# Fused attention and ternary feed-forward kernel: second norm from sums, a reordered opening, right-tap products on ScalarE and other moves in the last slots

## The chip, the cores and the metric

The kernel runs on 1 core of a Trainium2 chip. The metric is the device time of one execution in microseconds (us). PE is TensorE, DVE is VectorE, ACT is ScalarE, POOL is GpSimd and SP is the engine that issues all DMAs here.

## The reference, cut to what matters

```python
# x: (4, 2048, 512) float32, ctx: (4, 154, 512), 16 heads of 32, hidden width 2048
x = x + xattn(layernorm(x), ctx, ctx, Wq, bq, Wk, bk, Wv, bv, Wo, bo)  # causal mask, key > query is masked
x = x + ffn(layernorm(x), w1, conv_w, conv_b, w2)

def act_quant(x):
    scale = 127.0 / clip(max(abs(x), axis=-1), 1e-05)
    return clip(round(x * scale), -128, 127) / scale
def weight_quant(w):
    scale = 1.0 / clip(mean(abs(w)), 1e-05)
    return clip(round(w * scale), -1, 1) / scale
def ffn(x):
    h = act_quant(x) @ weight_quant(w1).T        # 512 -> 2048
    h = depthwise_conv1d(h, conv_w, pad=1) + conv_b   # 3 taps along the sequence
    h = silu(h)
    return act_quant(h) @ weight_quant(w2).T     # 2048 -> 512
```

## The kernel before, in words

The 8192 rows are cut into 16 blocks of 512 (`NB = 16`, four per batch). A software pipeline runs over slots `s = -1 .. 17`. In slot `s` the kernel makes the first norm and the queries of block `s + 1` (`do_q`), the attention, the output projection, the residual and the second norm of block `s` (`do_a`), the first feed-forward product, the three taps and Silu of block `s - 1` (`do_f`), and the second feed-forward product and result of block `s - 2` (`do_m`). Each engine has its own instruction list in program order; the lists are written out by hand, and counted semaphores tie them together. No planner orders anything.

A slot has a tile loop over 16 hidden tiles of 128 channels (`c = 0 .. 15`). For each tile PE multiplies (`mm1`, L867), DVE turns the bank into float32 (`dequant`, L1575), ACT copies the two edge columns and makes the left tap (`neighbours`, `tap0`, L1263), DVE adds the middle tap (`taps`, L1650), and the right tap is a product and a sum on POOL (L642, L644) or, for a few tiles, one DVE instruction (L1654). `TAP` and `SCALE` say which tiles go to POOL. The ring `g` has four buffers, so `dequant(c)` waits for the right tap of tile `c - 4`. PE fills the loop with the scores (L830, L836) and the products with the values (L861) of the attention; ACT has the exponentials (L1244).

Behind the loop comes the tail of the slot, with which the change deals. PE projects the queries (L679), turns the attention output (`turn_o`, L949), projects it (`project_out`, L959; four row tiles, one after another), turns the maxima of Silu (`turn_pm`, L1021), and makes the second product of block `s - 2` (`mm2`, L1043). DVE makes the low halves of the attention output (`at_low`, L1713), the maxima over the hidden tiles (`absmax`, L1659), and then for each of four row tiles `residual` (L1720) with its `bn_stats` (L1723) and `bn_aggr` (L1725). ACT centres each tile (`centre`, L1325) and DVE takes its largest absolute value (`centred_max`, L1729). `norm2` adds epsilon, POOL raises to the power -1/2 (L658), and `quantise` makes the scales in some ten instructions on 4 columns. `scales2` makes the scales of the second product from `turn_pm`; `spread_scales` (L1027) and `r2_copy` spread them, and POOL multiplies (`scaled`, L654) while ACT rounds (`rounded`, L1165). ACT quantises the rows (`hlq`, L1425).

DVE then makes the low halves of the queries (`q_low`, L1696), two results (`result`, L1777) and 16 maxima of the query scores (`maximum`, L1738), one for each `query_scores` of PE (L978). Among these 16 steps PE puts the rest of `mm2`. The slot ends with `turn_xq` (L1004), `spread_row` (L1013) and the first two tiles of `mm1` for the next slot. `offset` preloads a bank of the second product (ACT).

```python
def turn_pm():
    pe.wait_ge(pm_ok, at(s, 3, 2 if s == NB else 0))
    if do_a:
        pe.wait_ge(x2_ok, at(s, TT, 3))
```

In slot -1 the low halves of the queries alternate on DVE with the absolute sums of the weights `w1` (`w_abssum`, L1502), whose total PE spreads (`w_sums`, L763). In slot 0 ACT turns the weights `w2` into float16 (`w2_half`) between the centrings. In slot 16 (`s == NB`) the rows at the seams between blocks, 36 of them, are computed once more with their right neighbours in small instructions (`fix_...`); `fix_mm2` (L914) stands on PE right ahead of the last `mm2` in slot 17 (L1145).

## Time and profile before

| | |
|---|---|
| median of 3 runs | 1595.4 us (1593.45 to 1602.17) |
| profiled execution, its own time | 1609.67 us |
| its span in the trace | 1607.9 us |
| mean granted TensorE clock | 0.953 of full speed |
| busy: PE, DVE, ACT, POOL | 1486.2, 1353.2, 1146.0, 1032.0 us |

Busy time is a sum over the span; what one slot waits for is read from the chain of waits, which follows the work that ended last back to what released it. All times in the rows are microseconds from the start of the span, unless marked as mean ns.

### The profile page before, as it was taken

What the parts mean: (1) busy time and instruction counts of PE and PEld (TensorE: products, weight loads), DVE (VectorE), ACT (ScalarE), POOL (GpSimd) and SP (SyncE); (2) the same over time, 40 slices, a digit from 0 to 9 for tenths busy, and PEclk for the clock granted to TensorE, in tenths of its full rate; (3) what the DMA queues carried; (4) which work ended last, traced back from release to release, by engine and by line L of the source; (5) the groups of instructions that cost most, each with busy time, mean ns of one, the idle gap of its engine ahead of it and who ended that gap; (6) DMA issues with size and microseconds to landing.
All of it is one profiled execution on the core that took longest, in us unless ns stands there. A gap on an engine that the chain in (4) does not pass through costs nothing.

```text
span 1607.9 us, 24773 instructions
## 1 busy us (share of the span) xinstructions
PE 1486.2 (92%) x9097; PEld 906.9 (56%) x9097; DVE 1353.2 (84%) x2078; ACT 1146.0 (71%) x2028; POOL 1032.0 (64%) x838
## 2 busy tenths in 40 slices
PE   9799797999999999999999999999999999998776
PEld 6377364746565564747465665647474656655322
DVE  7565788798988989898889889897979898878896
ACT  3445596968688795959587787959586877878552
POOL 4101186768587685858586876858575867868462
PEclk8967799999999999999999999999999999999987
DMA  8540201012130303021220303031310302020000
GB/s 258 138 137 33 67 8 41 27 36 69 27 93 7 93 8 93 8 53 47 52 66 7 93 8 93 8 86 23 67 41 9 91 8 67 8 67 1 30 27 27
DMA packets 80343, 85.21 MB, mean 53 GB/s; under 512 B 29983, under 2 KB 55839, under 8 KB 79709
## 3 DMA queue, kind: packets, MB, share of 16 engines
q1 hardware_dynamic: 80221, 83.62, 19.2%
q8 instruction: 72, 1.18, 0.3%
q14 instruction: 50, 0.41, 0.1%
HBM read 38.74 MB, written 19.42 MB: 36 GB/s over the span
## 4 chain that ended last, share of the span: by engine, by line
PE 40%; DVE 36%; ACT 18%; issue 4%; POOL 3%; DMA 0%; DVEq 0%; ACTq 0%; SPq 0%
PE ps L861 12%; DVE negm L1738 10%; PE ps L867 8%; PE ps L1043 5%; ACT h L1268 4%; DVE r L1659 4%; DVE pm L1659 4%; ACT hqb L1165 3%; ACT h L1263 3%; ACT pexp L1244 3%; PE ps L830 3%; DVE h L1650 3%; DVE xn L1713 2%; DVE xr L1720 2%; PE ps L679 2%
## 5 line engine op out<-in xcount | busy, mean ns | idle before, releaser
L654 POOL TENSOR_TENSOR h<-h,r 128x512 f32<-128x512 f32 x240 | 306.9, 1327 | 102.4 <-ACT r L1165 102.4
L644 POOL TENSOR_TENSOR h<-h,gall 128x512 f32<-128x512 f32 x235 | 344.1, 1464 | 18.4
L642 POOL TENSOR_TENSOR gall<-gall,cw 128x512 f32<-128x512 f32 x235 | 257.5, 1096 | 118.8 <-DVE h L1650 118.8
L1650 DVE SCALAR_TENSOR_TENSOR h<-gall,cw,h 128x512 f32<-128x512 f32 x256 | 265.6, 1040 | 58.2 <-ACT h L1263 58.0
L861 PEld LDWEIGHTS ps<-va,pexp 128*128 128x128 f32 x2048 | 269.7, 198 | 30.1 <-issue 13.1
L861 PE MATMUL ps<-va,pexp 128*128 128x33 f32 x2048 | 267.3, 276 | 0.0
L867 PE MATMUL ps<-xqT,w1T 128*128 128x512 f16 x1024 | 257.7, 382 | 7.7 <-DVE gall L1575 7.4
L1575 DVE SCALAR_TENSOR_TENSOR gall<-ps,bias,srow 128x512 f32<-128x512 f32 x256 | 191.1, 747 | 79.0 <-POOL h L644 48.0
L1043 PE MATMUL ps<-w2T,hqb 128*128 128x512 fp8e4 x960 | 249.8, 390 | 0.0
L1244 ACT ACTIVATE pexp<-ps 128x512 f32<-128x512 f32 x320 | 179.7, 588 | 70.2 <-PE ps L830 27.9
L1263 ACT ACTIVATE h<-gall,cb,cw 128x512 f32<-128x512 f32 x256 | 221.9, 867 | 8.5
L1738 DVE TENSOR_REDUCE negm<-ps 128x4 f16<-128x616 f32 x256 | 186.6, 791 | 17.3 <-PE ps L981 8.4
L1165 ACT ACTIVATE hqb<-h 128x512 f16<-128x512 f32 x276 | 172.3, 683 | 40.3 <-PE ps L1043 23.4
L679 PE MATMUL ps<-hl,WqT 128*128 128x512 f16 x768 | 170.8, 379 | 2.6 <-DVE hl L1692 2.6
L1268 ACT ACTIVATE h<-h 128x512 f32<-128x512 f32 x256 | 155.3, 681 | 12.2 <-POOL h L644 11.9
L959 PE MATMUL ps<-WoT,pexp 128*128 128x512 f16 x512 | 156.0, 381 | 2.9 <-DVE xn L1713 2.9
L867 PEld LDWEIGHTS ps<-xqT,w1T 128*128 128x128 fp8e4 x1024 | 102.1, 112 | 86.3 <-DVE gall L1575 11.6
L1043 PEld LDWEIGHTS ps<-w2T,hqb 128*128 128x128 f16 x960 | 95.7, 100 | 88.6 <-issue 14.4
L1325 ACT ACTIVATE xn<-xr,mv 128x512 f32<-128x512 f32 x64 | 46.2, 722 | 126.9 <-DVE mv L1725 126.6
L978 PE MATMUL ps<-kB,hl 128*128 128x308 f16 x512 | 120.2, 309 | 14.2 <-DVE hl L1696 7.8
L658 POOL TENSOR_TENSOR nw<-nw,mhalf 128x4 f32<-128x4 f32 x16 | 16.3, 1019 | 175.2 <-DVE nw L1748 175.2
L679 PEld LDWEIGHTS ps<-hl,WqT 128*128 128x128 f16 x768 | 74.5, 98 | 91.0 <-issue 7.5
(220 smaller groups left out, 2328.2 us busy)
## 6 DMA issues: line engine op xcount, KB each, us to landing
qs<-hl SPq DMA_DIRECT2D x192, 128.0 KB, 2.6
xr<-in_x SPq DMA_DIRECT2D x16, 1024.0 KB, 5.5
out<-xr SPq DMA_DIRECT2D x64, 256.0 KB
h<-in_L_ffn_w SPq DMA_DIRECT2D x8, 1024.0 KB, 5.5
srow<-in_L_xattn_bo SPq DMA_DIRECT2D x15, 256.0 KB, 3.2
kst<-kh_scratch SPq DMA_DIRECT2D x32, 38.5 KB
xr<-in_ctx SPq DMA_DIRECT2D x1, 1024.0 KB
h<-in_L_xattn_Wk SPq DMA_DIRECT2D x1, 1024.0 KB, 8.4
```

Of the source, the lines that this page charges most:

```text
L642: gp.tensor_tensor(right, right, cw[:, c, 2:3].to_broadcast([P, TB]), ALU.mult).then_inc(c2m_ok, 1)
L644: gp.tensor_tensor(hc(c), hc(c), right, ALU.add).then_inc(c2p_ok, 1)
L654: gp.tensor_tensor(hc(c), hc(c), r2[:], ALU.mult).then_inc(u_ok, 1)
L679: r = mm(bank, a, b_, start=i == 0, stop=i == n - 1, **kw)
L861: r = mm(o, pr[:, t * P:(t + 1) * P], rhs, start=j == 0 and t % 2 == 0, stop=j == J, skip_group_check=True)
L867: r = mm(F[(c + 1) % 2], w1T[:, k, c * P:(c + 1) * P], xqT[:, k, :], start=k == 0, stop=k == KT - 1)
L1043: r = mm(bank, hq(c)[:, i * P:(i + 1) * P], w2T[:, c, :], start=False, stop=c == CT - 1, skip_group_check=late_results(s))
L1165: return nc.scalar.activation(o, i, ACT.Copy, **kw)
L1244: nc.scalar.activation(pexp[:, i % 3, :], A[i % 2], ACT.Exp, scale=1.0 / QS).then_inc(e_ok, 1)
L1263: nc.scalar.activation(hc(c), g[:, c % 4, 0:TB], ACT.Identity, bias=cb[:, c:c + 1], scale=cw[:, c, 0:1]).then_inc(c0_ok, 1)
L1650: ve.scalar_tensor_tensor(out=hc(c), in0=g[:, c % 4, 1:TB + 1], scalar=cw[:, c, 1:2], in1=hc(c), op0=ALU.mult, op1=ALU.add).then_inc(c1_ok, 1)
L1738: ve.tensor_reduce(negm[:, i, k * J:(k + 1) * J].rearrange("p (b e) -> p b e", b=2), banks, AX.X, ALU.max, negate=True).then_inc(mx_ok, 1)
```

## The change

- The second norm: `residual` also writes the sum of each row (`sum2`, an accumulator output); `bn_stats` and `bn_aggr` are gone. ACT centres with the sum, `512 * (mean - x)`, in four different quarters of `xn`, and a new `square` on ACT sums the squares (`sq2`). `norm2` and `quantise` divide by 512.
- DVE's order in the tail: three residuals, a maximum, the fourth residual, a maximum, `scales2`, two maxima; then, from slot 1 on, two `q_low`, `norm2`, two `q_low`, `quantise`. In slot 0 `q_low` stands ahead of the residuals, and eight of the 16 `maximum` ahead of `quantise`. In slot -1 the four `w_abssum` stand ahead of the four `q_low`.
- ACT in slot 0: `w2_half` stands behind the quantising of the rows. `offset` stands at other places among `centre` and `square`.
- Slot 15: `attention(3)`, `turn_o`, `at_high` and `at_low` are made inside the tile loop, in banks `A[0..3]`.
- Slot 16: the right-tap product of 15 tiles is on ACT and the sum on POOL (10 tiles had both on POOL); all 16 `scaled` are on DVE (6 were on POOL); the seam rows come one or two tiles sooner, and `fix_mm2` stands ahead of `turn_pm`, `fix_scales` ahead of `absmax_last`.

The diff, cut to its core (declarations of buffers and semaphores and renamed banks are left out):

```diff
@@ -129,8 +129,8 @@
 nb1 = sb("nb1", [P, TT], F32)
-st2 = sb("st2", [P, TT, 6], F32)
-mv2 = sb("mv2", [P, TT, 2], F32)
+sum2 = sb("sum2", [P, TT], F32)
+sq2 = sb("sq2", [P, TT], F32)
 nw2 = sb("nw2", [P, 4, TT], F32)
@@ -197,7 +200,7 @@
-    return xn[:, 2 + i % 2, :]
+    return xn[:, (i + 2) % 4, :]
@@ -381,8 +384,8 @@
-TAP = Share((0, 1, 2, 3, 4, 5, 6, 8, 9, 10, 11, 12, 13, 14, 15), last=(0, 2, 3, 5, 6, 8, 9, 11, 12, 14))
-SCALE = Share(tuple(range(CT)), last_but_one=(0, 1, 3, 4, 6, 7, 9, 10, 12, 14), last=(1, 4, 7, 10, 12, 14))
+TAP = Share((0, 1, 2, 3, 4, 5, 6, 8, 9, 10, 11, 12, 13, 14, 15), last=tuple(range(CT - 1)))
+SCALE = Share(tuple(range(CT)), last_but_one=(0, 1, 3, 4, 6, 7, 9, 10, 12, 14), last=())
 def early(s):
@@ -632,15 +635,18 @@
                 gp.tensor_tensor(nw1[:, 1, :], nw1[:, 0, :], mhalf[:], ALU.pow).then_inc(pw1, 1)
-            if s == NB and c == 4:
+            if s == NB and c == 3:
                 pool.wait_ge(fx_dve, 3)
...
-                pool.wait_ge(c1_ok, at(s, CT, c + 1 - CT))
                 right = g[:, c % 4, 2:TB + 2]
-                gp.tensor_tensor(right, right, cw[:, c, 2:3].to_broadcast([P, TB]), ALU.mult).then_inc(c2m_ok, 1)
-                pool.wait_ge(c2m_ok, TAP.done(s, c))
+                if s == NB:
+                    pool.wait_ge(c2a_ok, c + 1)
+                else:
+                    pool.wait_ge(c1_ok, at(s, CT, c + 1 - CT))
+                    gp.tensor_tensor(right, right, cw[:, c, 2:3].to_broadcast([P, TB]), ALU.mult).then_inc(c2m_ok, 1)
+                    pool.wait_ge(c2m_ok, TAP.done(s, c))
                 gp.tensor_tensor(hc(c), hc(c), right, ALU.add).then_inc(c2p_ok, 1)
@@ -940,13 +946,13 @@
             for k in range(NG):
-                if k == 2 and do_f:
+                if k == 2 and do_f and s != NB - 1:
                     pe.wait_ge(g_ok, at(s, CT, 0))
...
                 for t in range(TT):
-                    r = tp(OT[k][:, t * P:(t + 1) * P], osb[:, k, t * P:(t + 1) * P], identf[:])
+                    r = tp(obt(s, k)[:, t * P:(t + 1) * P], osb[:, k, t * P:(t + 1) * P], identf[:])
                 r.then_inc(ot_ok, 1)
@@ -955,6 +961,8 @@
             bank = OB[i]
+            if s == NB - 1 and i == 2 and k == 0:
+                pe.wait_ge(g_ok, at(s, CT, 0))
             for n, (a, part) in enumerate(((0, ah), (0, al), (1, ah))):
@@ -1049,6 +1057,8 @@
         for c in range(CT):
+            if s == NB - 1 and c == 14:
+                turn_o()
             if do_f and c >= 2:
@@ -1063,15 +1073,15 @@
                 mm2((c - 8) // 2)
-            if s == NB and c == 9:
+            if s == NB and c == 8:
                 fix_turn()
-            if s == NB and c == 11:
+            if s == NB and c == 10:
                 fix_mm1()
...
                 turn_x(range(KT))
-            if do_a and c == LASTU + 2:
+            if do_a and c == (LASTU + 1 if s == NB - 1 else LASTU + 2):
                 pv(NS - 2)
@@ -1082,7 +1092,7 @@
                 project_q(k)
-            if do_a and k == 1:
+            if do_a and k == 1 and s != NB - 1:
                 turn_o()
@@ -1094,6 +1104,7 @@
             fix_scales()
+            fix_mm2()
         if do_f:
@@ -1145,8 +1156,6 @@
                         r.then_inc(y_ok, 1)
-        if s == NB:
-            fix_mm2()
         if do_q:
@@ -1262,6 +1271,11 @@
+
+        def right_tap(c):
+            act.wait_ge(c1_ok, at(s, CT, c + 1 - CT))
+            right = g[:, c % 4, 2:TB + 2]
+            copy(right, right, scale=cw[:, c, 2:3]).then_inc(c2a_ok, 1)
@@ -1319,10 +1333,16 @@
-            act.wait_ge(ag_ok, at(s, TT, i + 1))
-            if i >= 2:
-                act.wait_ge(za_ok, at(s, TT, i - 1))
-            nc.scalar.activation(centred(i), ring(s)[:, i, :], ACT.Identity, bias=mv2[:, i, 0:1], scale=-1.0).then_inc(zx_ok, 1)
+            act.wait_ge(x2_ok, at(s, TT, i + 1))
+            if i == 2:
+                act.wait_ge(op_ok, at(s, TT, TT))
+            nc.scalar.activation(centred(i), ring(s)[:, i, :], ACT.Identity, bias=sum2[:, i:i + 1],
+                                 scale=-float(D)).then_inc(zx_ok, 1)
+
+        def square(i):
+            act.wait_ge(zx_ok, at(s, TT, i + 1))
+            nc.scalar.activation(osb[:, i, :], centred(i), ACT.Square, scale=1.0 / D,
+                                 accum_out=sq2[:, i:i + 1]).then_inc(sv_ok, 1)
@@ -1348,14 +1368,14 @@
         for c in range(CT + 1):
-            if s == NB and c == 8:
+            if s == NB and c == 7:
                 act.wait_ge(fx_dve, 12)
                 nc.scalar.activation(fxq, fxr, ACT.Copy, bias=HALF, scale=fq[:, 3:4]).then_inc(fx_act, 1)
-            if s == NB and c == 11:
+            if s == NB and c == 9:
                 act.wait_ge(fx_pe, 2)
...
                 copy(fsr, A[1][:, 0:N3]).then_inc(fx_act, 1)
-            if s == NB and c == CT:
+            if s == NB and c == 14:
                 act.wait_ge(fx_dve, 18)
@@ -1370,11 +1390,16 @@
                 tap0(c - 1)
+                if s == NB and c >= 2:
+                    right_tap(c - 2)
             if do_q and do_a and c in (9, 10):
...
                     x_high(k)
+            if s == NB - 1 and c == 15:
+                for k in range(NG):
+                    at_high(k)
             if do_f and do_a and LASTU < c < CT:
@@ -1385,7 +1410,7 @@
                 w_round(1, i)
-        if do_a:
+        if do_a and s != NB - 1:
             for k in range(NG):
@@ -1404,13 +1429,19 @@
                 w_round(0, i)
-        for i in range(TT):
-            if s == 0:
-                w2_half(i)
-            if do_a:
-                centre(i)
-            if late_results(s) and i != 2:
-                offset((0, 1, 2, 2)[i])
+        if do_a:
+            centre(0)
+            if late_results(s):
+                offset(0)
+            centre(1)
+            centre(2)
+            centre(3)
+            if late_results(s):
+                offset(1)
+            for i in range(TT):
+                square(i)
+            if late_results(s):
+                offset(2)
         if s == 1:
@@ -1424,6 +1455,9 @@
                                      scale=qm1[:, 3, i:i + 1]).then_inc(xq_ok, 1)
+        if s == 0:
+            for i in range(KT):
+                w2_half(i)
         if late_results(s):
@@ -1718,11 +1752,7 @@
             ve.scalar_tensor_tensor(out=ring(s)[:, i, :], in0=OB[i], scalar=1.0 / WS, in1=ring(s)[:, i, :],
-                                    op0=ALU.mult, op1=ALU.add).then_inc(x2_ok, 1)
-            dve.wait_ge(x2_ok, at(s, TT, i + 1))
-            ve.bn_stats(st2[:, i, :], ring(s)[:, i, :]).then_inc(bn_ok, 1)
-            dve.wait_ge(bn_ok, at(s, TT, i + 1))
-            ve.bn_aggr(mv2[:, i, :], st2[:, i, :]).then_inc(ag_ok, 1)
+                                    op0=ALU.mult, op1=ALU.add, accum_out=sum2[:, i:i + 1]).then_inc(x2_ok, 1)
@@ -1744,8 +1774,8 @@
         def norm2():
-            dve.wait_ge(ag_ok, at(s, TT, TT))
-            ve.tensor_scalar(nw2[:, 0, :], mv2[:, :, 1], EPS, None, ALU.add).then_inc(ln2, 1)
+            dve.wait_ge(sv_ok, at(s, TT, TT))
+            ve.tensor_scalar(nw2[:, 0, :], sq2[:], 1.0 / D, EPS, ALU.mult, ALU.add).then_inc(ln2, 1)
@@ -1754,7 +1784,8 @@
             dve.wait_ge(za_ok, at(s, TT, TT))
-            ve.tensor_tensor(qm1[:, 0, :], qx[:], nw2[:, 2, :], ALU.mult).then_inc(ln2, 1)
+            ve.scalar_tensor_tensor(out=qm1[:, 0, :], in0=qx[:], scalar=1.0 / D, in1=nw2[:, 2, :],
+                                    op0=ALU.mult, op1=ALU.mult).then_inc(ln2, 1)
             dve.wait_ge(ln2, at(s, 10, 5))
@@ -1764,7 +1795,7 @@
             dve.wait_ge(ln2, at(s, 10, 8))
-            ve.scalar_tensor_tensor(out=qb[:, 0, :], in0=mv2[:, :, 0], scalar=-1.0, in1=qm1[:, 3, :],
+            ve.scalar_tensor_tensor(out=qb[:, 0, :], in0=sum2[:], scalar=-1.0 / D, in1=qm1[:, 3, :],
                                     op0=ALU.mult, op1=ALU.mult).then_inc(ln2, 1)
@@ -1806,15 +1837,22 @@
                 fix_stats()
-            if s == NB and c == 7:
+            if s == NB and c == 6:
                 fix_quantise()
-            if s == NB and c == 14:
+            if s == NB and c == 12:
                 fix_conv()
+            if s == NB and c == 16:
+                fix_absmax()
             if do_q and do_a and c == 0:
...
                 x_low(1)
+            if s == NB - 1 and c == 13:
+                attention(3)
+            if s == NB - 1 and c == 16:
+                for k in range(NG):
+                    at_low(k)
             if do_f and c < CT:
@@ -1830,21 +1868,21 @@
                 w_scales(1)
-            if do_a and c in (4, 7, 10, 14):
+            if do_a and c in ((4, 7, 10) if s == NB - 1 else (4, 7, 10, 14)):
                 attention((c - 4) // 3)
         if s == NB:
+            fix_scales()
             absmax_last(0, 4, pm)
-            fix_absmax()
+            fix_scaled()
             absmax_last(4, 6, r2)
             merge_last(r2, 2)
-            fix_scales()
             absmax_last(6, 8, pexp[:, 0, :])
...
                 w_limit(1, i)
-        if do_a:
+        if do_a and s != NB - 1:
             for k in range(NG):
@@ -1853,26 +1891,39 @@
             merge()
+        if s == 0:
+            for k in range(NG):
+                q_low(k)
         if do_a:
...
             residual(1)
+            residual(2)
             centred_max(0)
-            residual(2)
+            residual(3)
             centred_max(1)
-            residual(3)
-            norm2()
         if do_f:
...
             centred_max(3)
+        if s > 0 and do_q:
+            q_low(0)
+            q_low(1)
+        if do_a:
+            norm2()
+        if s > 0 and do_q:
+            q_low(2)
+            q_low(3)
+        if s == 0:
+            for n in range(8):
+                maximum(n // NG, n % NG)
+        if do_a:
             quantise()
-        if do_q:
+        if s == -1:
             for k in range(NG):
-                if s == -1:
-                    w_abssum(0, k)
+                w_abssum(0, k)
+            for k in range(NG):
                 q_low(k)
-        if s == -1:
             w_scales(0)
@@ -1885,17 +1936,15 @@
         if s == NB:
-            fix_scaled()
+            fix_result()
             for c in SCALE.dve(s):
                 scaled(c)
-        for n in range(TT * NG):
+        for n in range(8 if s == 0 else 0, TT * NG):
             if do_q:
...
             result(3)
-        if s == NB:
-            fix_result()
         if s == NB + 1:
```

## Rows read from the trace of the kernel before

**Rows 1.** The page, busy us (share of the span) xinstructions.

```profile
PE 1486.2 (92%) x9097; PEld 906.9 (56%) x9097; DVE 1353.2 (84%) x2078; ACT 1146.0 (71%) x2028; POOL 1032.0 (64%) x838
```

**Rows 2.** Chain of waits, tail of slot 9: start us, us, what.

```profile
961.80 0.69 DVE xr L1720
...
963.35 0.69 DVE xr L1720
...
977.53 11.38 DVE negm L1738 x16
```

**Rows 3.** Timeline of DVE there: start us, us, instruction [idle before].

```profile
962.52 0.69 DVE L1723 BATCH_NORM_STATS2 st<-xr 128x6 f32<-128x512 f32 x1
...
964.89 0.65 DVE L1729 TENSOR_REDUCE qx<-xn 128x1 f32<-128x512 f32 x1
...
973.49 2.72 DVE L1696 SCALAR_TENSOR_TENSOR hl<-ps,bqc,hl 128x512 f16<-128x512 f32 x4
```

**Rows 4.** Timeline of PE there.

```profile
966.29 0.63 PE L1021 MATMUL ps<-identf,pm 128*128 128x128 f32 x4 [2.09 <-DVE xr L1720]
966.75 7.07 PE L1043 MATMUL ps<-w2T,hqb 128*128 128x512 fp8e4 x32
...
976.36 0.42 PE L978 MATMUL ps<-kB,hl 128*128 128x308 f16 x2
```

**Rows 5.** Timeline of ACT there.

```profile
940.00 1.28 ACT L1268 ACT_TABLE_LOAD   x1
...
963.47 0.72 ACT L1325 ACTIVATE xn<-xr,mv 128x512 f32<-128x512 f32 x1 [5.65 <-DVE mv L1725]
```

**Rows 6.** Windows of slots 9 and 3: busy us of each engine, granted clock, DMA.

```profile
966.20:974.00 7.80, 7.71 (x40) 4.05 (x41) 7.32 (x25) 1.95 (x4) 1.02 (x1) 1.00 0.01 3
...
432.50:441.10 8.60, 8.60 (x35) 3.63 (x33) 8.12 (x27) 1.93 (x3) 1.02 (x1) 0.80 0.00 0
```

**Rows 7.** Timelines of DVE, PE and SP in slot -1.

```profile
63.88 0.75 DVE L1696 SCALAR_TENSOR_TENSOR hl<-ps,bqc,hl 128x512 f16<-128x512 f32 x1 [10.21 <-ACT hl L1319]
64.55 2.28 DVE L1502 TENSOR_REDUCE wsum<-h 128x4 f32<-128x2048 f32 x1
...
72.79 0.59 PE L763 MATMUL ps<-mw,onesf 128*128 128x1 f32 x2 [6.76 <-DVE mw L1506]
...
73.47 7.84 SPq L532 DMA_DIRECT2D qs<-hl  x12
```

**Rows 8.** Timelines of ACT and PE, tail of slot 0.

```profile
158.64 1.93 ACT L1165 ACTIVATE hqb<-h 128x2048 f16<-128x2048 f32 x1
...
171.51 3.36 ACT L1425 ACTIVATE osb<-xr,qb,qm 128x512 f16<-128x512 f32 x4 [2.42 <-DVE qb L1770]
...
174.25 1.19 PE L978 MATMUL ps<-kB,hl 128*128 128x308 f16 x4 [7.59 <-DVE hl L1696]
...
189.46 1.89 PE L867 MATMUL ps<-xqT,w1T 128*128 128x512 f16 x8
```

**Rows 9.** Timelines of POOL, PE and DVE, slots 16 and 17.

```profile
1527.40 1.04 POOL L642 TENSOR_TENSOR gall<-gall,cw 128x512 f32<-128x512 f32 x1 [2.73 <-DVE h L1650]
1528.52 1.62 POOL L644 TENSOR_TENSOR h<-h,gall 128x512 f32<-128x512 f32 x1
...
1555.98 1.03 PE L867 MATMUL ps<-xqT,w1T 128*128 128x512 f16 x4
...
1566.11 4.40 DVE L1668 TENSOR_REDUCE pm<-h 128x512 f32<-128x4096 f32 x1
...
1573.13 0.69 DVE L1673 TENSOR_TENSOR pm<-pm,r 128x512 f32<-128x512 f32 x1
...
1582.79 5.48 PE L914 MATMUL ps<-w2T,xn 128*12 128x512 fp8e4 x16
...
1583.01 12.72 DVE L1744 TENSOR_TENSOR h<-h,r 128x512 f32<-128x512 f32 x10 [2.54 <-ACT r L1165]
...
1589.17 13.99 PE L1145 MATMUL ps<-w2T,hqb 128*128 128x512 fp8e4 x64
```

11 lines of the change are left out of this document (6 added, 5 removed).

## The prediction

> **What bounds the kernel now.** I began with the page: PE is busy for 92% of the span and DVE for 84% [rows 1], so no engine alone is the limit, and what counts is where PE stands still. The chain of waits over one slot in the middle comes next. It runs on PE through the tile loop, passes to ACT and DVE at its end, and stays on DVE from `at_low` to the last `maximum`. In the tail of slot 9 it steps from residual to residual, 1.55 us apart (961.80 to 963.35), and reaches the first of 16 query maxima at 977.53, 15.7 us after the first residual [rows 2]. The timelines of the engines say what PE does meanwhile: 2.09 us of standstill ahead of `turn_pm`, released by the third residual at 966.29, then 7.07 us of `mm2`, and the first query scores at 976.36 [rows 4]. ACT waits 5.65 us for the first centring [rows 5]. So the tail is DVE's, and PE has its largest hole there; 13 slots (2 to 14) have this tail. The windows show a second price: the stretch of `mm2` in slot 9 has a granted clock of 1.00 (2.4 GHz), that of slot 3 has 0.80, a part of it at 1.2 GHz, behind the same standstill [rows 6]. I asked for that window in slots 2 to 14; six of the 13 (3, 6, 7, 10, 11, 14) look like slot 3.
>
> The median of the runs is 1595.4 us, the profiled execution took 1609.67 (span 1607.9): 14.3 above the median. I make the sum against the profiled one and take it off the median too.
>
> **Steady tail, slots 2 to 14.** Removed from DVE: four `bn_stats` of 0.69 us [rows 3] with `bn_aggr` and their waits. A residual alone takes 0.68 to 0.69, so 1.55 - 0.68 = 0.87 each, 3.5 in all [rows 2]. Added to DVE: the accumulator output of four residuals. No row shows one. It is bounded below by nothing and above by another pass as long as `bn_stats`, 0.69; I take 0.1, since the sum goes along with a pass that runs anyway, so 0.4 in all. DVE would start its maxima 3.1 earlier, at 974.4.
>
> PE: `turn_pm` waits for the third residual. Three residuals follow each other without a break now, done at 961.80 + 3 x 0.78 = 964.1, and PE has finished `project_out` at 966.29 - 2.09 = 964.2. So the standstill goes, and the first scores come at 976.36 - 2.09 = 974.3, done at about 974.6. Each side would have held the other before 974.4 to 974.6. The maxima start at 974.6 in place of 977.53: 2.9 us. Their 16 steps (11.38 us [rows 2]) keep pace with PE, so the end of the slot moves by as much. I take 2.6, because POOL starts to scale only 2.1 earlier and so works 0.8 further into the next slot, and `norm1` waits there for its power on POOL.
>
> The cover of what is added: ACT gets four squares. With 0.72 each, as a centring [rows 5], and the last residual at 965.4, centring, offset and squares end at 965.4 + 0.72 + 0.6 + 2.9 = 969.6; the power on POOL takes 1.0 [rows 6], so `quantise` can begin near 971. DVE is busy to there with `scales2`, two maxima and four `q_low` (2.72 [rows 3]), which were behind it and are now its cover. If each square took 0.3 more, the wait would show by about 1 us. 13 x 2.6 = 33.8 us (bounds 13 x 0.2 = 3, with 0.69 for each accumulator output, and 13 x 2.9 = 38).
>
> On the accumulator output a page has something to say. The Trainium skill ("VectorE: DVE Perf Modes", section "Two Vector instructions with no wait between them") says that an op which writes out its accumulator is two instructions, the main one and a read. No row here shows the second. By it the 0.1 would be the length of a small instruction that overlaps its neighbour, and the sum would stay.
>
> **Clock in six of these slots.** The stretch takes 8.60 against 7.07 [rows 4, 6], 1.5 on PE; about half of it is hidden today because DVE is later anyway. If the clock stays up once the standstill is gone, each of the six gives 0.8 more: 5 us (0 to 9).
>
> **Slot -1.** DVE waits 10.21 us for the first query half and then alternates four `q_low` with three `w_abssum` of 2.28 us; PE stands still for 6.76 [rows 7]. The four sums' weights were asked for on SP long before, right behind the key projections, so the three sums fit into the 10.21, and the queries are complete 3 x 2.28 = 6.8 earlier. What is late next are the 12 query transfers (7.84 us on SP [rows 7]), which start by as much earlier behind the fetch of the values. I take 7 with a warmer PE (4 to 9).
>
> **Slot 0.** PE waits 7.59 us for `q_low` [rows 8]; now it can go on at 166.7. But `norm2` waits for the fourth square (near 170.7), eight maxima (5.7) and `quantise` (ten small instructions, 1.8 as an estimate) follow, and ACT quantises the rows at 178.4 where it did at 171.51 [rows 8]. Behind these 3.4 us now stand the four `w2_half`, 1.93 each at first [rows 8] and 7.5 together, which used to lie among the centrings. Behind them wait the transposed maxima, the copies of `xqT` and with them `mm1`, and SP's transfers of the maxima. 178.4 + 3.4 + 7.5 + 2.5 = 191.8, against 189.46 [rows 8]. I take a loss of 2.2 (loss 4 to gain 3, if the maxima are faster than I think). Slot 1: centring and squares end about 1 us before today's last centring, and ACT's copies of w2 follow them: 1 us (0 to 1.5).
>
> **Slot 15.** `at_low` leaves the tail, but Silu of the last tile, fed by POOL, holds the second `absmax` as before. The residuals are the same as in the middle; PE will have stood still longer before them, so I take 1.5 of the 2.1 on PE (0 to 2.4).
>
> **Slots 16 and 17.** POOL's 1.04 for the product leaves its 2.7 us per tile [rows 9]; ACT's pitch becomes about 2.1, an estimate from four instructions per tile. But PE has four `mm2` between its last eight tiles and ended at 1555.98, 10 us before the maxima at 1566.11 [rows 9]: DVE made `fix_conv` just there. With that block earlier I take 4.5 us (0 to 7). Behind the scales, `fix_mm2` (5.48 us) keeps PE from the last `mm2` until 1589.17, though the scales were ready at 1583.0 [rows 9]. Moved, it lies beside `absmax_last`, and the last `mm2` starts some 1.5 after the scales: 4.7. The scaling is all on DVE: 12.72 / 10 = 1.27 each beside POOL [rows 9]; alone I take 0.69, as the only other product of two such tiles without POOL [rows 9], 11 us for 16, which hides under 13.99 of PE. If it stayed at 1.27 it would take 20 and cost 6. PE is colder at the start of the last `mm2`: -1.7. Sum for the end: 7.5 (2 to 11).
>
> **Sum.** 33.8 + 5 + 7 - 2.2 + 1 + 1.5 + 7.5 = 53.6 us. Against its own time 1609.7 - 53.6 = 1556.1; off the median 1595.4 - 53.6 = 1541.8, say 1542.
>
> **The rivals.** First, the squares or their table hold `quantise`. ACT loads a table once in 1.28 us ahead of Silu [rows 5]; if the square were in another one, each of 15 slots would have 1.28 more on the way to the quantised rows, of which some 0.2 is hidden: 15 to 16 us, 1558. Against it: copies and centrings cause no load today. Beside that mechanism stands the Trainium skill ("ScalarE: Activation LUTs", section "Table sets: the hidden batching unit"): a function outside the loaded set costs a switch, and its list of cheap functions that every set has does not name the square. By that rule the time is this rival's. Second, the accumulator output costs another pass, 0.69 in place of 0.1: 13 x 2.4 = 31 less, 1573. Third, the next tile loop takes half of the steady gain back, by POOL's backlog: 1559.
>
> On the other side, slower than before: the accumulator output breaks the pace of the residual. The other terms give 19.8 us, so the kernel is slower once a tail loses more than 1.4 us. That needs 4 x e > 2.9 + 1.4, e above 1.1 us per residual, 1.8 for one that takes 0.68. With three times 0.68 (e = 1.4) the tail loses 2.7, 14 slots lose 38, and the time is 1613. Against it: no row of DVE on 512 columns here takes much over its 0.68 but where POOL is busy beside it.
>
> **How the numbers follow.** Forecast 0.55 (its own range 1530 to 1555); table or squares 0.15; second pass 0.1; backlog 0.1; slower 0.04; better than the forecast, because slot 0's loop also runs at the higher clock, 0.06 (1525). The range from 1526 to 1572 leaves out the second pass in part, the slower case and the best one. A measurement of this kernel tells about 0.5%, 8 us, from no change. Faster by more: 0.94; within: 0.02; slower: 0.04.
>
> **What would show it.** Right: no standstill of PE ahead of `turn_pm` (L1021); residuals 0.7 to 0.8 apart; the first query maximum 12.8 us after the first residual; granted clock 1.00 in all 13 stretches of `mm2`; query scores of slot -1 some 7 us earlier; w2's halves ahead of `mm1` at the end of slot 0; the last `mm2` within 2 us of the scales. Wrong: a table load ahead of the squares, an accumulator row of 0.5 us or more, DVE waiting for the squares at `norm2`, or PE waiting for DVE in the tile loop where it did not.

## The result: 45 us faster, and where they came from

The changed kernel takes 1552.9 us (median of 4 runs, 1551.3 to 1559.2); the kernel before took 1598.2 on the same chip (4 runs, 1593.5 to 1602.2; the prediction had the first three of them, with a median of 1595.4). The ratio is 0.9725 with a 95% interval of 0.9684 to 0.9767. Between the medians lie 45.3 us. The profiled execution took 1552.53 us, its span is 1550.8, against 1607.9 before: 57.1 us between the two spans, of which 11.4 belong to a clock that happened to be low in one of them, as shown below.

The page first: PE's busy share rose from 92% to 94%, with the same 9097 instructions; DVE lost 67 us of work and ACT took on 45.

```profile
PE 1463.2 (94%) x9097; PEld 895.0 (58%) x9097; DVE 1286.2 (83%) x2015; ACT 1191.2 (77%) x2171; POOL 1020.6 (66%) x827
```

**The steady tail.** The chain of waits over the tail of slot 9 now runs on PE from `project_out` to the first query scores, and changes to DVE only there (before, DVE had it throughout [rows 2]).

```profile
926.14 0.44 PE ps L1029 x4
926.58 6.91 PE ps L1051 x32
...
936.10 0.28 PE ps L986 x2
...
936.40 11.47 DVE negm L1768 x16
```

The timeline of DVE in the same tail gives the pace of the residuals and what the accumulator costs:

```profile
923.80 0.68 DVE L1754 SCALAR_TENSOR_TENSOR xr<-ps,xr 128x512 f32<-128x512 f32 x1
924.41 0.08 DVE L1754 DVE_READ_ACCUMULATOR xr<-ps,xr 128x1 f32 x1
924.41 0.69 DVE L1754 SCALAR_TENSOR_TENSOR xr<-ps,xr 128x512 f32<-128x512 f32 x1
...
931.26 0.16 DVE L1778 TENSOR_SCALAR nw<-sq 128x4 f32<-128x4 f32 x1
...
936.40 11.46 DVE L1768 TENSOR_REDUCE negm<-ps 128x4 f16<-128x616 f32 x16 [0.69 <-PE ps L986]
```

Residuals follow each other every 0.61 us, where they were 1.55 apart [rows 2]. The read of the accumulator begins when the next residual begins. From the first residual to the first query maximum it is 12.6 us, before 15.7. The maxima now wait 0.69 for PE: PE is now the later of the two. ACT's timeline shows the squares, one every 0.61 us, and no table load ahead of them; `norm2` (L1778) finds them ready:

```profile
928.10 0.61 ACT L1344 ACTIVATE osb<-xn 128x512 f32<-128x512 f32 x1
928.62 0.19 ACT L1344 ACTIVATION_READ_ACCUMULATOR osb<-xn 128x1 f32 x1
```

The waits of PE over slots 2 to 14 (waiting line, releaser, sum, times, longest) had this row at the top before:

```profile
PE ps L1021 <- DVE xr L1720: 25.6, 13, 2.6
```

After, `turn_pm` has no row there, and these are the first two:

```profile
PE ps L1000 <- DVE negm L1768: 7.7, 13, 0.6
PE ps L836 <- ACT pexp L1253: 5.9, 13, 0.5
```

The window of `mm2` in slot 3, whose clock was 0.80 [rows 6], has 1.00:

```profile
411.00:418.50 7.50, 7.50 (x38) 3.68 (x37) 7.40 (x20) 6.18 (x15) 0.94 (x1) 1.00 0.00 1
```

Taken from one `spread_row` to the next, slots 2 to 14 shrank from 1152.9 to 1110.0 us, 42.9. The six slots that I had named for their clock gave 3.9 to 4.3 each, six of the others 2.7 to 3.0, slot 2 gave 1.7.

**The opening.** DVE makes all four sums while it would have waited (51.26), and the query halves follow at 63.75, so the query scores of slot -1 begin at 66.63 in place of 73.54. SP's transfers move by less than that because the fetch of the values stands ahead of them (71.74 against 73.47 [rows 7]), and the last ones, of the maxima, come right behind (80.33 against 86.22). The first scores of slot 0 begin 7.2 us earlier, 83.6 against 90.8. What they wait for has changed: before, PE came to them straight from its own work, held up by the query maxima on DVE; now they wait 0.95 for the transfers of the maxima, so SP's queue is the bound there.

```profile
51.26 8.85 DVE L1536 TENSOR_REDUCE wsum<-h 128x4 f32<-128x2048 f32 x4
...
63.75 2.73 DVE L1730 SCALAR_TENSOR_TENSOR hl<-ps,bqc,hl 128x512 f16<-128x512 f32 x4 [3.43 <-ACT hl L1333]
```

**Slot 0.** Its tail, from `turn_x` to `spread_row`, takes 2.3 us longer. ACT stands still for 8.09 us until DVE has quantised the rows, and only then makes the four halves of `w2`. PE waits 5.32 for the copy of the maxima behind them:

```profile
160.04 3.36 ACT L1456 ACTIVATE osb<-xr,qb,qm 128x512 f16<-128x512 f32 x4 [8.09 <-DVE qb L1801]
163.27 7.28 ACT L1174 ACTIVATE hqb<-h 128x2048 f16<-128x2048 f32 x4
170.46 0.46 ACT L1174 ACTIVATE negmT<-ps 16x384 f16<-16x384 f16 x1
```

**The end.** Slots 15, 16 and 17 together gave nothing. Slot 15 became 1.3 us longer: `turn_pm` waits 2.78 for the residuals (PE had finished `project_out` long before), and `mm2(0)` behind it runs at the low clock, 16 products in 6.08 us.

```profile
1435.01 1.08 PE L1029 MATMUL ps<-identf,pm 128*128 128x128 f32 x4 [2.78 <-DVE xr L1754]
...
1436.57 6.08 PE L1051 MATMUL ps<-w2T,hqb 128*128 128x512 fp8e4 x16
```

The tile loop of slot 16, from the first `dequant` to the first `absmax_last`, takes 54.2 us, 4.6 more than the 49.6 before. Of these 4.6, 1.2 are work that only changed its place: `fix_absmax` and `fix_scales` stood behind the first `absmax_last` and now stand ahead of it. In this stretch DVE has 6.8 us less work with the taps, and it stands still for 17.3 us in place of 6.8. DVE's timeline has the three waits that do most of it, for POOL's power of the seam rows and twice for `mm1`; PE's timeline shows `mm2(0)` in 5.23 us between two `mm1`, where the later ones take 3.63:

```profile
1473.76 0.15 DVE L1622 TENSOR_TENSOR xn<-xn 36x1 f32<-36x1 f32 x1 [1.71 <-POOL xn L640]
...
1485.98 0.75 DVE L1609 SCALAR_TENSOR_TENSOR gall<-ps,bias,srow 128x512 f32<-128x512 f32 x1 [4.58 <-PE ps L873]
...
1493.18 0.75 DVE L1609 SCALAR_TENSOR_TENSOR gall<-ps,bias,srow 128x512 f32<-128x512 f32 x1 [3.11 <-PE ps L873]
...
1513.04 4.40 DVE L1702 TENSOR_REDUCE pm<-h 128x512 f32<-128x4096 f32 x1
```

```profile
1479.23 5.23 PE L1051 MATMUL ps<-w2T,hqb 128*128 128x512 fp8e4 x16
...
1486.98 3.63 PE L1051 MATMUL ps<-w2T,hqb 128*128 128x512 fp8e4 x16
...
1518.66 5.98 PE L920 MATMUL ps<-w2T,xn 128*12 128x512 fp8e4 x16
...
1530.39 3.96 PE L1156 MATMUL ps<-w2T,hqb 128*128 128x512 fp8e4 x10 [1.51 <-ACT hqb L1174]
```

The move of `fix_mm2` did what it should: it lies beside `absmax_last` (1518.66), and the last `mm2` starts 17.35 us after the first `absmax_last` where it took 23.06, 5.7 less; it then takes 1.6 longer (15.62 against 13.99 [rows 9]) because it starts at the low clock.

**The sum of what the traces show:** 7.2 - 2.3 - 0.3 (slot 1) + 42.9 - 1.3 - 0.5 = 45.7 us, close to the 45.3 of the medians; with runs of one kernel that differ by 8 us and more, an agreement as close as this is partly chance. The other 11.4 between the two profiled spans lie in the tile loop of slot 0, where PE was busy nearly all the time in both (41.74 of 42 us before) and its granted clock was not the same. The window of before there:

```profile
92.00:134.00 42.00, 41.74 (x274) 36.72 (x275) 23.25 (x38) 20.92 (x38) 1.93 (x1) 0.55 0.40 138
```

### The profile page after: what moved, and what is told of

Read it like the earlier page. It is cut to its first block, busy times and chain, and to the rows that moved or that the text cites. A ratio compares the mean times of both kernels' runs of the same rounds, so it can differ in the third digit from the quotient of the medians.

```text
span 1550.8 us, 24827 instructions
## 1 busy us (share of the span) xinstructions
PE 1463.2 (94%) x9097; PEld 895.0 (58%) x9097; DVE 1286.2 (83%) x2015; ACT 1191.2 (77%) x2171; POOL 1020.6 (66%) x827
## 4 chain that ended last, share of the span: by engine, by line
PE 68%; DVE 16%; ACT 10%; issue 3%; SPq 2%; POOL 1%; DMA 1%; DVEq 0%; ACTq 0%
PE ps L867 13%; PE ps L685 11%; PE ps L873 10%; PE ps L967 10%; DVE negm L1768 9%; PE ps L1051 9%; ACT hqb L1174 4%; ACT pexp L1253 3%; PE ps L836 3%; PE ps L955 2%; DVE h L1684 2%; PE ps L933 1%; PE ps L1021 1%; PE ps L842 1%; PE ps L1035 1%
## 5 line engine op out<-in xcount | busy, mean ns | idle before, releaser
L650 POOL TENSOR_TENSOR h<-h,gall 128x512 f32<-128x512 f32 x240 | 354.7, 1478 | 45.9 <-ACT gall L1174 28.3
L660 POOL TENSOR_TENSOR h<-h,r 128x512 f32<-128x512 f32 x234 | 296.7, 1312 | 46.4 <-ACT r L1174 46.4
L648 POOL TENSOR_TENSOR gall<-gall,cw 128x512 f32<-128x512 f32 x225 | 246.6, 1096 | 91.9 <-DVE h L1684 91.9
L1684 DVE SCALAR_TENSOR_TENSOR h<-gall,cw,h 128x512 f32<-128x512 f32 x256 | 259.5, 1016 | 48.6 <-ACT h L1272 48.3
L867 PEld LDWEIGHTS ps<-va,pexp 128*128 128x128 f32 x2048 | 263.3, 194 | 29.1 <-issue 11.4
L867 PE MATMUL ps<-va,pexp 128*128 128x33 f32 x2048 | 261.2, 272 | 0.0
L1051 PE MATMUL ps<-w2T,hqb 128*128 128x512 fp8e4 x960 | 244.2, 384 | 0.0
L685 PEld LDWEIGHTS ps<-hl,WqT 128*128 128x128 f16 x768 | 74.3, 98 | 91.2 <-issue 7.7
L1339 ACT ACTIVATE xn<-xr,sum 128x512 f32<-128x512 f32 x64 | 44.0, 716 | 80.7 <-DVE xr L1754 74.2
```

Of the source, the lines that this page charges most:

```text
L648: gp.tensor_tensor(right, right, cw[:, c, 2:3].to_broadcast([P, TB]), ALU.mult).then_inc(c2m_ok, 1)
L650: gp.tensor_tensor(hc(c), hc(c), right, ALU.add).then_inc(c2p_ok, 1)
L660: gp.tensor_tensor(hc(c), hc(c), r2[:], ALU.mult).then_inc(u_ok, 1)
L685: r = mm(bank, a, b_, start=i == 0, stop=i == n - 1, **kw)
L867: r = mm(o, pr[:, t * P:(t + 1) * P], rhs, start=j == 0 and t % 2 == 0, stop=j == J, skip_group_check=True)
L1051: r = mm(bank, hq(c)[:, i * P:(i + 1) * P], w2T[:, c, :], start=False, stop=c == CT - 1, skip_group_check=late_results(s))
```

## The experiments

Each kernel ran beside the kernel before, and all ratios are against it. Times vary by up to some 15 us between runs of one kernel; in the traces the clock in slot 0 makes most of such a difference. So I read each edit in its own stretch of the trace. The stretches that an edit does not touch repeat well: slots 2 to 14 took 1109.7 to 1110.2 us in ten of the eleven traces with the changed tail, the changed kernel's among them (the eleventh, four taps, is told below). Stretches used below: slot 0's tail (`turn_x` to `spread_row`); slot 15 (`spread_row` to `spread_row`); the loop of slot 16 (first `dequant` to first `absmax_last`); the end (last `spread_row` to DVE's last result). Where the first `absmax_last` itself was moved, the loop has no number. The loops of "before" and "end undone" leave out the 1.2 us of `fix_absmax` and `fix_scales` that the other numbers hold.

| kernel | median us | ratio (95%) | slot 0 tail | slots 2-14 | slot 15 | loop 16 | end |
|---|---|---|---|---|---|---|---|
| before | 1598.2 | 1 | 50.4 | 1152.9 | 77.0 | 49.6 | 95.4 |
| changed | 1552.9 | 0.9725 | 52.7 | 1110.0 | 78.3 | 54.2 | 95.9 |
| end undone | 1549.3 | 0.9693 (0.9632-0.9754) | 54.9 | 1109.8 | 74.9 | 50.5 | 96.1 |
| taps on POOL | 1553.7 | 0.9697 (0.9651-0.9743) | 54.7 | 1109.9 | 76.8 | 56.1 | 97.9 |
| slot 15 old | 1554.3 | 0.9686 (0.9613-0.9759) | 52.3 | 1109.8 | 74.9 | 53.7 | 95.1 |
| early w2_half | 1548.0 | 0.9671 (0.9609-0.9732) | 46.8 | 1109.7 | 76.8 | 54.0 | 95.5 |
| old order | 1595.5 | 0.9957 (0.9928-0.9987) | 54.6 | 1151.8 | 78.6 | 53.9 | 95.4 |
| bn_stats kept | 1589.9 | 0.9935 (0.9908-0.9961) | 54.1 | 1145.3 | 80.0 | 54.1 | 95.7 |
| seams old | 1556.2 (1 run) | | 54.7 | 1110.2 | 76.7 | 54.6 | 96.9 |
| mm2 in halves | 1543.7 | 0.9645 (0.959-0.9701) | 49.8 | 1110.2 | 74.6 | 51.7 | 93.7 |
| mixed end | 1538.1 | 0.9608 (0.9568-0.9649) | 49.8 | 1109.9 | 74.6 | 48.9 | 90.5 |
| maximum in loop | 1536.9 | 0.9602 (0.9557-0.9647) | 46.8 | 1109.8 | 74.6 | | 91.2 |
| old opening | 1564.2 | 0.9773 (0.9721-0.9825) | 52.1 | 1109.9 | 75.1 | 53.5 | 94.7 |
| four taps | 1538.5 | 0.9585 (0.9551-0.9618) | 49.5 | 1118.2 | 75.1 | 51.0 | 91.9 |

### The steady tail: order or instructions?

**Old order.** The sums and squares stay; DVE's order in slots 1 to 15 is that of before.

```diff
 residual(1)
-residual(2)
 centred_max(0)
-residual(3)
+residual(2)
 centred_max(1)
+residual(3)
+norm2()
 scales2()
 centred_max(2); centred_max(3)
-q_low(0); q_low(1); norm2(); q_low(2); q_low(3)
 quantise()
+q_low(0); q_low(1); q_low(2); q_low(3)
```

> The changed kernel with the norm by sums kept, but DVE's order in the tail of slots 1 to 15 as before: a maximum between the residuals, norm2 right behind the last residual, q_low behind quantise. Theory A (the order is half of the gain: norm2 then stands waiting for the fourth square while scales2, two maxima and q_low would be its cover): DVE stands 2.5 to 3.5 us at norm2 in each slot, slots 2 to 14 take 1145 to 1155 where the changed kernel takes 1110, time 1590 to 1598. Rival (the gain is the removed bn_stats alone, the order is free): slots 2 to 14 within 5 us of 1110.

Theory A: slots 2 to 14 took 1151.8, the median was 1595.5. The whole steady gain but 1.1 us is gone, though `bn_stats` is gone too. DVE's timeline of slot 9 says where it went:

```profile
951.38 0.68 DVE L1754 SCALAR_TENSOR_TENSOR xr<-ps,xr 128x512 f32<-128x512 f32 x1
...
955.82 0.17 DVE L1778 TENSOR_SCALAR nw<-sq 128x4 f32<-128x4 f32 x1 [3.75 <-ACT osb L1344]
...
964.03 2.20 DVE L1768 TENSOR_REDUCE negm<-ps 128x4 f16<-128x616 f32 x3
```

`norm2` stands right behind the last residual and waits 3.75 us for the fourth square, a little more than the 2.5 to 3.5 expected. All that could have covered the wait is queued behind it. From the first residual (948.09) to the first maximum it is 15.9 us, where the kernel before has 15.7.

**bn_stats kept.** The new order, but each residual is followed by `bn_stats` and `bn_aggr`, and ACT makes no squares.

```diff
-... op0=ALU.mult, op1=ALU.add, accum_out=sum2[:, i:i + 1]).then_inc(x2_ok, 1)
+... op0=ALU.mult, op1=ALU.add).then_inc(x2_ok, 1)
+ve.bn_stats(st2[:, i, :], ring(s)[:, i, :]).then_inc(bn_ok, 1)
+ve.bn_aggr(mv2[:, i, :], st2[:, i, :]).then_inc(ag_ok, 1)
```

> The changed kernel with its new order, but bn_stats and bn_aggr behind each residual and no squares, so the norm comes as before. Theory A (removed instructions and their waits carry most of the steady gain): residuals 1.5 us apart again, PE stands before turn_pm, slots 2 to 14 take 1135 to 1150, time 1578 to 1593. Rival (the order carries it: the third residual is 0.7 sooner and q_low covers): slots 2 to 14 at most 1125, time below 1570.

Theory A again: 1145.3. The residuals are 1.54 apart and PE stands before `turn_pm`:

```profile
947.47 0.63 PE L1033 MATMUL ps<-identf,pm 128*128 128x128 f32 x4 [1.51 <-DVE xr L1756]
947.94 7.37 PE L1055 MATMUL ps<-w2T,hqb 128*128 128x512 fp8e4 x32
```

The two halves of the edit do not add up. The sums alone give 1152.9 - 1151.8 = 1.1 us, the order alone 1152.9 - 1145.3 = 7.6, both together 42.9: 34 of the 43 us need both. And what each gives alone is the clock. In both kernels PE has the full clock over slots 2 to 14 (bn_stats kept, then old order), where the kernel before had fallen to half for a few microseconds in six slots (each row: window, its length, PE's busy time, granted clock, DMA share and GB/s):

```profile
265.23:1410.56 1145.33, 1100.42 (x6869) 1.00 0.18 47
265.49:1417.29 1151.80, 1098.63 (x6869) 1.00 0.18 47
```

In these six slots the order alone gives 7.0 us and the sums alone 4.4. In the other seven, which had the full clock before too, the order alone gives 0.6, the sums alone lose 3.4, and both together give 18.8. So without the clock neither half is worth anything. The sums take DVE's 3.5 us away and put a latency of four squares in their place; only the order hides that latency.

### The opening

**Old opening.** In slot -1 sums and halves alternate again; all else is as changed.

```diff
 for k in range(NG):
     w_abssum(0, k)
-for k in range(NG):
     q_low(k)
```

> The changed kernel with the sums of w1 alternating with q_low in slot -1, as before. Theory A (my term of 7 us is DVE's order alone): the first query scores of slot -1 at 73.5 in place of 66.6, the first scores of slot 0 some 7 us later, 1559 to 1561 with the same clock in slot 0's loop. Rival (the fetch of the values on SP and the transfers of the queries set the end of slot -1): the first scores of slot 0 move by under 3 us.

Theory A: the query scores begin at 73.7 in place of 66.6, the first scores of slot 0 at 91.1 in place of 83.6, and the lowest run is 7.7 us above the changed kernel's lowest (1559.0 against 1551.3). The median is 11.3 above, because two of its four runs had a mean clock of 0.954 and 0.955, the others 0.965. Its trace is one of those with a low clock in slot 0's loop (below). Whether the old opening makes that more frequent is not settled by four runs.

**Early w2_half.** In slot 0 the four halves stand between the squares and the quantising of the rows.

```diff
+if s == 0:
+    for i in range(KT): w2_half(i)
 act.wait_ge(ln2, at(s, 10, 10))
 for i in range(TT): ...   # hlq
-if s == 0:
-    for i in range(KT): w2_half(i)
```

> The changed kernel with the four w2_half of slot 0 between the squares and the quantising of the rows on ACT, where ACT stands still for 8.09 us. Theory A (they are all that holds the transposed maxima and mm1): slot 0 ends 5 to 7 us earlier, 1546 to 1548. Theory B (the low clock of PE in this stretch, or the transfers of the maxima, hold mm1 anyway): under 2 us.

```profile
148.40 7.29 ACT L1174 ACTIVATE hqb<-h 128x2048 f16<-128x2048 f32 x4
156.57 3.36 ACT L1459 ACTIVATE osb<-xr,qb,qm 128x512 f16<-128x512 f32 x4 [0.89 <-DVE qb L1801]
160.74 0.48 ACT L1174 ACTIVATE negmT<-ps 16x384 f16<-16x384 f16 x1 [0.81 <-PE ps L1000]
```

The halves fit into the 8.09 us, with 0.89 left over, and the rows are quantised no later: 19.0 us after the first residual in both kernels. The tail took 46.8, 5.9 less, as theory A said. The four later kernels with this edit took 46.8 to 49.8, the eight changed kernels with the halves behind 52.1 to 54.9; the means, this run with its four followers, are 48.5 and 53.8.

### The end

**End undone.** Slots 15 to 17 as before, the rest as changed: the parts of the change that name these slots, reversed. Its core:

```diff
-if s == NB - 1 and c == 14: turn_o()
+if do_a and k == 1: turn_o()
-last=tuple(range(CT - 1)))
+last=(0, 2, 3, 5, 6, 8, 9, 11, 12, 14))
-last_but_one=(0, 1, 3, 4, 6, 7, 9, 10, 12, 14), last=())
+last_but_one=(0, 1, 3, 4, 6, 7, 9, 10, 12, 14), last=(1, 4, 7, 10, 12, 14))
-if s == NB: fix_turn_pm(); fix_scales(); fix_mm2()   # ahead of turn_pm
+if s == NB: fix_turn_pm(); fix_scales()
+if s == NB: fix_mm2()                                # ahead of the last mm2
```

> The changed kernel with everything of slots 15 to 17 as it was before (attention and turn_o of slot 15, right taps and scalings on POOL, seam rows and fix_mm2 at their old places); norm by sums, order of the tail, slots -1 and 0 as changed. Theory A (the end as changed gains nothing, what fix_mm2 gives back is lost in the tile loop of slot 16): within 2 us of the changed kernel, 1551 to 1553; first dequant to last absmax in slot 16 near 49.7 where the changed kernel has 54.2, last mm2 5 to 6 later. Theory B (the end gains the 9 us of my sum and the gain was lost elsewhere): 1561 or more.

Theory A, and a little more: 1549.3, where the theory said 1551 to 1553. Slot 15 is 3.4 us shorter, the loop of slot 16 3.7 (1.2 of them moved work), and the last `mm2` starts 5.5 later. All of the change's edits in the last three slots together are worth nothing; by the two traces they cost 3.2 us.

**Taps on POOL.** In slot 16 `TAP.last` is that of before, and POOL makes product and sum.

```diff
-last=tuple(range(CT - 1)))
+last=(0, 2, 3, 5, 6, 8, 9, 11, 12, 14))
-if s == NB and c >= 2: right_tap(c - 2)
```

> The changed kernel with the right-tap product of slot 16 back on POOL for ten tiles and six right taps on DVE; all else of the end as changed. Theory A (the product on ACT lengthens the chain from one ring buffer to the next, so the ring of four sets the pace): the loop of slot 16 falls from 54.2 to about 50 and the time by 4, to 1549. Theory C (the loop is slow because of mm2 and the seam rows at the low clock, wherever the taps are): the loop stays at 54 and the time at 1553.

My theory A fell: the loop took 56.1 us, 1.9 longer, not 4 shorter. The time, 1553.7, is that of theory C, though its loop was to stay at 54. With the rest of the end as changed, the product is better on ACT.

**Seams old.** The seam rows' steps of slot 16 at their old tiles.

```diff
-if s == NB and c == 8: fix_turn()      # PE
+if s == NB and c == 9: fix_turn()
-if s == NB and c == 6: fix_quantise()  # DVE
+if s == NB and c == 7: fix_quantise()
-if s == NB and c == 12: fix_conv()     # and so for fix_mm1, the copies, the power
+if s == NB and c == 14: fix_conv()
```

> The changed kernel with the seam rows of slot 16 one or two tiles later, where they were (fix_turn, fix_mm1, fix_quantise, fix_conv, their copies and Silu); taps on ACT and the moved fix_mm2 as changed. After the run with taps on POOL, whose loop took 56.1 us, the taps are not the cause. Theory C1 (fix_turn lies with mm2(0) between two products of the loop, and earlier seam rows stop DVE while the queue of PE is empty and its clock low): the loop falls from 54.2 to 48 to 50. Theory C2 (the wait for mm2(0) at the low clock alone): it stays at 53 to 55.

C1 fell too: the loop took 54.6, within the 53 to 55 of C2. Each of the two alone leaves the loop at 54 to 56, both together, with the other edits of the end undone as well, bring it to 50.5 (51.7 with the moved work). What the three slow loops share is seen in DVE's waits: 1.70 to 1.72 us for POOL's power, where the end undone has 0.45, and 8.6 (taps on POOL), 5.8 (seams old) and 8.1 (changed) for `mm1` from the second such wait on, where the end undone has 0.79. In the end undone `fix_quantise` runs on DVE while PE makes `mm2(0)`, and the power is nearly ready. In the others DVE reaches `fix_quantise` 1.7 us before POOL has made its power, and `mm2(0)` begins 0.7 to 4.6 us later, counted from the first `dequant`. Which of the two costs how much no run takes apart.

**Slot 15 old.** The last attention, `turn_o`, `at_high` and `at_low` at their old places.

```diff
-if s == NB - 1 and c == 14: turn_o()
-if do_a and k == 1 and s != NB - 1: turn_o()
+if do_a and k == 1: turn_o()
```

> The changed kernel with slot 15's last attention, turn_o, at_high and at_low at their old places and in their old banks. Theory A (the moved attention leaves PE standing before turn_pm, and what follows runs at 1.2 GHz): 1 to 2 us faster than the changed kernel, mm2(0) in 3.6 to 4 us where it takes 6.1. Theory B (the move gains the 1.5 us of my sum): 1 to 2 slower than the changed kernel.

Slot 15 took 74.9, 3.4 less than changed. PE no longer stands still before `turn_pm`, and `mm2(0)` takes 3.63 us where it took 6.08, as theory A said. In five more traces with the old places it took 74.6 to 75.1 (old opening keeps the new ones, and took 75.1 as well); the other traces with the new places and the new norm took 76.7 to 78.6. So the move costs 1.6 to 3.7 us in most executions and nothing in one. That one, the old opening, separates the standstill from the clock. PE stands still for 3.34 us there, more than the 2.78 of the changed kernel, but the clock stays up, and `mm2(0)` has its short time:

```profile
1455.34 0.63 PE L1029 MATMUL ps<-identf,pm 128*128 128x128 f32 x4 [3.34 <-DVE xr L1754]
...
1456.22 3.63 PE L1051 MATMUL ps<-w2T,hqb 128*128 128x512 fp8e4 x16
```

`turn_pm` begins 61.0 us into the slot in both, and 60.8 with the old places: the residuals on DVE release it, and the move does not make them earlier. So the standstill itself costs nothing, and the loss is the low clock behind it. The measured time of slot 15 old says little: two of its four runs took 1562, two 1546, and the trace of the first kind has PE at half clock in slot 0's loop while busy the whole time:

```profile
95.00:130.00 35.00, 35.00 (x244) 0.50 0.27 96
```

The same stretch of the changed kernel:

```profile
95.00:130.00 35.00, 34.14 (x317) 0.88 0.28 99
```

**mm2 in halves.** With early w2_half and slot 15 old, and each `mm2` of slot 16 cut in two.

```diff
-if s == NB and c in (8, 10, 12, 14): mm2((c - 8) // 2)
+if s == NB and c >= 8: mm2((c - 8) // 2, range(8 * (c % 2), 8 * (c % 2) + 8))
```

> The changed kernel with three edits: w2_half early in slot 0 (as in its own run, 5.9 us there), slot 15 as before (as in its own run, 2 to 3 us), and new: the four mm2 of slot 16 cut in halves of eight products, one half behind each of the last eight tiles, where PE stands still 0.7 to 3.5 us per tile. Theory (DVE waits 4.58 and 3.11 us for mm1 behind a whole mm2): both waits fall under 1.5 us, the loop of slot 16 from 54.2 to 49 to 51, time 1538 to 1543. Rival (POOL's sum and the ring of four set the pace of the tiles anyway): the loop stays within 1.5 us of 54.2, time 1544 to 1546.

The loop took 51.7, 2.0 to 2.3 less than in slot 15 old and early w2_half (53.7, 54.0); DVE's waits for `mm1` are 1.89 and 2.74 where they were 4.58 and 3.11. The direction was the theory's, but the waits stayed above 1.5 and the loop outside the 49 to 51 that I expected. The median was 1543.7, a touch above the 1538 to 1543.

**Mixed end.** On top of that, the halves one tile sooner, `fix_quantise` back at tile 7 with its power still at tile 3, and six right taps as one DVE instruction.

```diff
-if s == NB and c >= 8: mm2((c - 8) // 2, range(8 * (c % 2), 8 * (c % 2) + 8))
+if s == NB and 7 <= c < 15: mm2((c - 7) // 2, range(8 * ((c - 7) % 2), 8 * ((c - 7) % 2) + 8))
-last=tuple(range(CT - 1)))
+last=tuple(c for c in range(CT) if c not in (1, 3, 5, 8, 11, 15)))
-if s == NB and c == 6: fix_quantise()
+if s == NB and c == 7: fix_quantise()
```

> The kernel with early w2_half, slot 15 as before and mm2 in halves, with three more edits in slot 16: the halves one tile sooner (tiles 7 to 14), fix_quantise one tile later than changed (tile 7, its power on POOL stays at tile 3), and six right taps (tiles 1, 3, 5, 8, 11, 15) as one DVE instruction, nine as a product on ACT and a sum on POOL. Theory (three waits set the loop: 1.19 us per early tile for POOL's sum, 1.70 for the power of the seam rows, 2 to 3 for mm1 behind mm2; the edits take each in part): first dequant to the first absmax_last in 46 to 48 us where mm2_split had 51.7 and before 49.7; slots 16 and 17 some 4 shorter, time 1536 to 1541. Rival (DVE becomes the bound with six more instructions of 0.75 us): 51 or more.

The loop took 48.9, a little above the 46 to 48 of the theory, the end 90.5, 5.4 less than the changed kernel; the median was 1538.1. In DVE's timeline `fix_quantise` follows the taps without a wait, and the waits for `mm1` are down to 0.94 and 1.23:

```profile
1465.84 0.75 DVE L1677 SCALAR_TENSOR_TENSOR h<-gall,cw,h 128x512 f32<-128x512 f32 x1
1466.51 0.14 DVE L1615 TENSOR_TENSOR xn<-xn 36x1 f32<-36x1 f32 x1
...
1475.27 0.75 DVE L1602 SCALAR_TENSOR_TENSOR gall<-ps,bias,srow 128x512 f32<-128x512 f32 x1 [0.94 <-PE ps L873]
...
1479.46 0.75 DVE L1602 SCALAR_TENSOR_TENSOR gall<-ps,bias,srow 128x512 f32<-128x512 f32 x1 [1.23 <-PE ps L873]
```

```profile
1465.42 2.16 PE L1049 MATMUL ps<-w2T,hqb 128*128 128x512 fp8e4 x8
1467.42 1.03 PE L873 MATMUL ps<-xqT,w1T 128*128 128x512 f16 x4
1468.28 1.89 PE L1049 MATMUL ps<-w2T,hqb 128*128 128x512 fp8e4 x8
```

**Maximum in the loop.** The first maximum at tile 14 in place of behind the loop.

```diff
+if s == NB and c == 14: absmax_last(0, 4, pm)
 ...
 if s == NB:
     fix_scales()
-    absmax_last(0, 4, pm)
     fix_scaled()
```

> The kernel end_mixed with absmax_last over the first eight tiles (4.4 us on DVE) at tile 14 inside the loop of slot 16, where it stood behind it. Theory A (DVE has waits to fill there): slots 16 and 17 become 1 to 3 us shorter than in end_mixed. Theory B (ring and taps of the last tiles wait for it, so it is only moved): within 1 us, or up to 2 longer.

Theory B: the end took 91.2 against 90.5. The 4.4 us were moved, not hidden. The median of 1536.9 is no gain over 1538.1: in this trace slot 0's tail was 3.0 shorter, which this edit does not touch.

**Four taps.** The mixed end with four DVE taps.

```diff
-last=tuple(c for c in range(CT) if c not in (1, 3, 5, 8, 11, 15)))
+last=tuple(c for c in range(CT) if c not in (3, 7, 11, 15)))
```

> The kernel end_mixed with four right taps of slot 16 on DVE (tiles 3, 7, 11, 15) in place of six. In end_mixed DVE hardly waits from tile 3 to tile 8. Theory A (DVE is now the bound of the loop of slot 16): 1.5 us less for the two instructions of 0.75 us, loop 47.4, slots 16 and 17 at 89, time 1536 to 1538. Theory B (the ring behind POOL's sums is next at the same pace): the loop within 0.7 us of 48.9 or longer, with waits of 1.2 us for POOL's sum back in the early tiles, time 1538 to 1541.

Theory B: the loop took 51.0, 2.1 longer, and two waits of 1.19 for POOL's sum are back; those for `mm1` behind `mm2` grew from 2.2 to 3.6. So the six taps on DVE were not its bound; they took load off the ring. The median was 1538.5 in six runs. Its trace also shows what one late transfer can cost. At the start of slot 6 PE waited for the transposed maxima, a wait of 0.96 that the trace of the mixed end does not have there, and the clock fell:

```profile
603.74 0.59 PE L836 MATMUL ps<-qs,kst 97*128 97x512 f16 x2 [0.96 <-DMA qs<-negmT]
```

```profile
600.00:605.00 5.00, 3.57 (x19) 1.00 0.31 109
605.00:610.00 5.00, 5.00 (x27) 0.61 0.64 210
...
615.00:620.00 5.00, 5.00 (x21) 0.53 0.00 0
620.00:625.00 5.00, 5.00 (x40) 1.00 0.00 0
```

That slot took 92.6 us in place of 84.4, and it is all that makes slots 2 to 14 longer in this trace.

## Why the prediction was right, and which of its steps failed

The forecast was 1542, within 1526 to 1572; it came to 1552.9, 11 above. By the medians the change gave 45.3 where the sum said 53.6. The mechanism of the largest term was right. That the total came so near has some luck in it: by the traces the steady tail gave 4.1 us more than its two terms, while slot 1, slot 15 and the end gave 12.1 less. The terms, one by one:

- **Steady tail, 33.8 + 5:** right in mechanism and close in size. 42.9 came, some 36 of them without the clock. PE's standstill before `turn_pm` went from 25.6 us in 13 slots to none. The first maximum came 12.6 us after the first residual, as forecast (12.8). The accumulator costs 0.08 us that the next instruction overlaps; I had taken 0.1. By the rule of the Trainium skill ("VectorE: DVE Perf Modes", section "Two Vector instructions with no wait between them"), an op with an accumulator output is a main instruction and a read; the trace agrees, with two rows for each residual. My step was incomplete in one thing: it put the gain on the removed instructions and named the order as their cover. The runs show 1.1 us for the first alone and 7.6 for the second alone, and these only by the clock.
- **Clock in six slots, 0.8 each:** right, and on these six slots. They gained about 1.2 more than the others, 7 in all where I took 5, and the clock is 1.00 over all of slots 2 to 14. (The 8.60 that I set against 7.07 was the length of a window; `mm2` itself took 8.76 in slot 3, so the 1.5 is nearly right.)
- **Slot -1, 7:** 7.2 came, and the run with the old opening took it back. The path was not as I had it: the query transfers start 1.7 us earlier, not 6.8, since the fetch of the values holds them. Before the change they did not hold slot 0 at all; PE and DVE did, and these were 6.9 earlier. That the transfers then took away no more than 0.95 is luck.
- **Slot 0, -2.2:** -2.3 in the trace. The four `w2_half` behind the rows were its cause; put in front, they gave 5 us back on average over the traces, since the wait for `quantise` covers them.
- **Slot 1, +1:** -0.3. Centring and squares did not end 1 us earlier: ACT's copies of `w2` behind them begin 68.4 us into the slot in both kernels. PE's spreading of the scales beside them lay wholly in the half clock, 2.02 us for 1.69 before.
- **Slot 15, +1.5:** wrong in sign. The step that failed is "PE will have stood still longer before them, so I take 1.5 of the 2.1 on PE". The earlier `project_out` saved nothing, because `turn_pm` waits for the residuals, which come no sooner; behind the longer standstill the clock fell, and `mm2(0)` took 6.08 us where its sixteen products take 3.63 at the high clock. With the old places the slot took 74.9. The new norm alone had given 2.1 there (77.0 to 74.9), and the move took 1.3 more than that back.
- **Slots 16 and 17, +7.5:** wrong, -0.5. The term that failed is "With that block earlier I take 4.5 us" for the tile loop: it became 4.6 longer, 3.4 without the moved work. I had one bound of the loop in view, POOL's 2.7 us per tile, and took it away. The next ones were as near: the power for the seam rows in POOL's queue, a whole `mm2` between two `mm1` at the low clock, and the sums of the ring. The term for `fix_mm2`, 4.7, was right (5.7 measured), so was that for the cold start of the last `mm2` (-1.7, measured -1.6), and the scaling takes 0.61 each on DVE without POOL (I had taken 0.69), so that it hides under PE and costs nothing, as the sum has it.

The first rival, a table load ahead of the squares, did not come. The table loads number 30 in both traces. The wait of `norm2` for the squares, which that rival would have brought in every slot, shows in slot 0 alone, 1.45 us. By the Trainium skill ("ScalarE: Activation LUTs", section "Table sets: the hidden batching unit") a square outside the loaded set would have cost a load. The page does not say which sets hold the square, so I gave it more weight than it has; the trace, with no load more, says that the square is in a set that this kernel loads anyway. The second pass for the accumulator, the slower case and the backlog of POOL did not come either: 42.9 / 13 = 3.3 us per slot arrived in full at the next `spread_row`. The best case, slot 0's loop at the higher clock, is true of the profiled pair (11.4 us) but, by times and clocks, not of a typical pair of runs.

The best kernels here, with early w2_half, slot 15 old and the mixed end, take 1537 to 1539: some 15 us less than the changed kernel, and 0.9608 (0.9568 to 0.9649) of the kernel before.

## What to carry to other kernels

When work moves to another engine, ask which instruction first needs its result and what stands in front of that instruction: here the move without a new order gave 1 us, the order without the move 8, both together 43. And look at the clock slot by slot before a small gain is put down to an edit: those of 1 and 8 came only from slots in which the clock no longer fell. Before one bound of a loop is removed, list the second and the third from the same stretch of the trace, or the edit only changes the name of the wait. A block that PE makes between two steps of a loop costs its length at the clock that PE has there, so cut it small and put the pieces into PE's pauses: halves in place of wholes made the loop of slot 16 2.0 to 2.3 us shorter.

## What the runs showed of the hardware

- **The clock can stay low under full load.** Near the start of slot 0's loop the granted clock fell to 0.50 in all fourteen traces, at 86 to 95 us. In eleven it came back after 7 to 10 us; in three (before, slot 15 old, old opening) it stayed at half for 37, 51 and 48 us, while PE was busy for 35.00 of the 35 us from 95 to 130. The loop up to `turn_x` then ends 64.5 to 66.8 us after the first query scores of slot -1, else 50.0 to 52.9. What decides between the two stays open.
- **A single short wait can cost eight times its length.** In one trace 0.96 us of waiting for a transfer, followed by some 14 us at half clock, made one slot 8.2 us longer. It need not: with `bn_stats` kept, PE stood still for 1.2 to 1.9 us before `turn_pm` in 11 of 13 slots, and the clock stayed up; 3.34 us in slot 15 of the old opening did not lower it either. What decides is open.
- **Accumulator outputs are nearly free.** On DVE the read takes 0.08 us and begins together with the next instruction; on ACT it takes 0.19, and squares of 512 columns still follow every 0.61 us.
- **DVE without POOL.** The product of a float32 tile of 512 columns takes 9.7 / 16 = 0.61 us on DVE when POOL does nothing beside it, 1.27 when POOL multiplies too [rows 9].
